# A macaron block on one core: the period of the first scores in an order of its own, and the first chunk's bias add and statistics moved

## The chip, the cores and the metric

The kernel runs on one core of a Trainium2 chip. The metric is the device time of one execution in microseconds (us); lower is better. Engines: PE (TensorE, matmuls), DVE (VectorE), ACT (ScalarE), POOL (GpSimd), and SP (SyncE), which here only issues DMAs. Each engine runs its own instructions strictly in their order; engines wait for each other on semaphores.

## The reference

The input x has 16 batches of 256 rows of 256 numbers. Three sublayers are added to it one after the other, each on the layer-normalised rows: half of a feed-forward, a causal attention with 16 heads of 16 and rotary positions, and half of the same feed-forward again.

```python
def ffn(x):                       # w1: 1024x256, w2: 256x1024, each quantised to -1, 0, 1
    h = gelu(x @ ternary(w1).T + b1)
    return h @ ternary(w2).T + b2
def ternary(w):                   # scale = mean(|w|), clip(round(w / scale), -1, 1)
    ...
x = x + 0.5 * ffn(layernorm(x))
x = x + attention(layernorm(x), Wq, Wk, Wv, Wo)      # softmax(rope(q) rope(k).T / 4, causal) v
x = x + 0.5 * ffn(layernorm(x))
```

## The kernel before, in words

All 4096 rows stay in SBUF in `res` (32 tiles of 128 rows). The kernel is three stages: feed-forward 0, attention, feed-forward 1.

**Feed-forward** goes by chunks of 512 rows. For a chunk, DVE makes `xn` (L147) from mean and rstd, which POOL works out in eight small instructions (`normaliser`, L116 to L132, called `moments`); PE transposes `xn` (L156), ACT and DVE split the transpose into a high and a low part (`xt_hi` L162, `xt_lo` L167), PE makes the hidden layer (L173) in 8 parts of 128 features, ACT applies gelu (L240), ACT or DVE rounds (`g_hi`), DVE takes the rest (`g_lo`, L257), and PE multiplies by `w2q` (L534): first for two of the four row tiles part by part as `g_lo` comes, then it transposes the next chunk's `xn`, then it does the other two tiles. POOL adds half of b2 to `res` (`residual`, L312); it may do so once the chunk's `xn` is made, and DVE adds PE's output only behind it.

**The first chunk** has the weights to quantise as well. DVE reduces |w1| (L344), PE spreads the mean over the partitions (`mean_of`, L497), DVE sets the threshold (L265, L267) and makes `w1q` in two halves (L355, L357), with `xt_lo` between them. ACT sums |w2| in four parts (L476); DVE adds these up (L362), waits for PE's second `mean_of`, which PE does behind the first two hidden parts, sets the second threshold, takes the statistics of chunk 1 (L142), and makes `w2q` in four pieces (L370, L372) between the first `g_lo`s. POOL waits for the first piece of `w1q`, does `residual(0)`, then `moments(1)`, then `residual(1)`.

**Attention** goes by periods p = -2, -1, 0, ..., 16, each in two halves h. Period p makes q and k of batch p+3 (`QK`, L670; `rope`, L677 and L680 on DVE; `rotate`, POOL L802; `top` L994, `take_rest` L889, `middle` L999 and `low` L807 split them into three bf16 parts, which SP stores to HBM, L686), makes v (`V`, L1158), normalises batch p+4 (`normalise`, L873; `XT`, L1171; `copy_xt`, L1008; `low_xt`, L912), makes the scores of batch p+1 only for their row maxima (`S`, 12 groups of L1057 and L1062 in a ring of three banks; `maxima`, DVE L860), splits and transposes the maxima (`split_max` POOL L789 to L795; `MT` PE L1138; `copy_max` ACT L1016; `max_rows` SP L756), and makes the scores of batch p again, transposed and with the maxima subtracted (`T`), with exponentials (L982) and the product with v (`PV`, L1118, L1121). SP loads q and k two periods ahead of `T` (`load`, L744), one half of the heads at a time, with `max_rows` and the stores in the same in-order queue. `normals` (POOL, the same eight instructions) serves two batches at once: it is done in every odd period behind `low`, from statistics that DVE takes in that period (L864). `MT` writes into the third bank of the scores' ring, so the next `S` in that bank waits for `copy_max`. The first scores are those of period -1 (`FIRST` is -2): there PE waits for their loads and only then goes on to `QK`.

Of the kernel before, what the change touches and what calls it, by code (L numbers as in the profile page):

```python
# [14 lines left out]
P = 128  # L15
# [3 lines left out]
FC = F // P  # L19
AHEAD, BEGUN = 7, 4  # L20
# [23 lines left out]
def macaron_kernel(nc, x, w1t, b1, w2t, b2, wqk, wv, wo, rope_cos, rope_sin, out):  # L44
    ctx = ExitStack()
    with ctx:
# [165 lines left out]
        def feed_forward(phase):  # L212
# [7 lines left out]
            with ExitStack() as stack:  # L220
# [78 lines left out]
                def gpsimd(pool):  # L299
                    if phase == 0:  # L300
                        constants(pool)
                        moments(pool, 0)
                        pool.wait_ge(bias_in, 32)
                        pool.tensor_scalar(b2h[:], b2f[:], 0.5, None, ALU.mult).then_inc(b2_ready, 1)

                        pool.wait_ge(b2_ready, 1)
                        pool.wait_ge(s_quant, 1)
# [8 lines left out]
                    if phase == 0:  # L316
                        moments(pool, 1)
                        residual(1)
                        for n, (hi, lo, full, _) in enumerate(att_weights):
                            pool.wait_ge(attw_hi, n + 1)  # L320
                            pool.tensor_tensor(lo[:], full[:], hi[:].bitcast(F32), ALU.subtract).then_inc(attw_lo, 1)
                        pool.wait_ge(attw_lo, len(att_weights))
# [13 lines left out]
                def vector(dve):  # L336
                    if phase == 0:
# [24 lines left out]
                        nc.vector.tensor_reduce(wtot[:, 1:2], wsum2[:], AX.X, ALU.add).then_inc(s_tot, 1)  # L362
                        threshold(1)
# [60 lines left out]
                    if phase == 0:  # L424
                        dve.wait_ge(x_in, 32)
                        ln_stats(1)
# [67 lines left out]
                def tensor(pe):  # L494
# [4 lines left out]

                    def first_qk(n):  # L500
                        pe.wait_ge(xt_hi_s, KC * n + KC)
                        pe.wait_ge(xt_lo_s, KC * n + KC)
                        for t in range(2):
                            qk_products(nc, banks[t], t, (wqk_hi, wqk_lo), [part[:, :, 0:SEQ] for part in (xt_hi, xt_lo)])\
                                .then_inc(turning.qk_ready, 1)
# [56 lines left out]
                    if phase == 0:  # L562
                        pe.wait_ge(const_ready, 15)
                        mean_of(0)
                        transpose_x(pe, 0)

# [124 lines left out]
def attention(nc, sem, banks, turning, res, wqk, wv, wo, cos_t, sin_t, ident, ident_b, mask_qk, mask_kq, minus_rows,  # L691
# [18 lines left out]
    with ExitStack() as ctx:  # L710
# [64 lines left out]
        def gpsimd(pool):  # L775
# [38 lines left out]
            def step(p, h):  # L814
                opening = p.known and p.p == FIRST
                if h == 0:
                    if opening:
                        normals(p)
                    if p.has(1):
                        pad(p)  # L820
                        split_max(p, 0)
                    if p.has(3):
                        rotate(p, 0)
                    if p.known and p.p == BATCH - 2:
                        moments(pool, following)
                else:
                    if p.has(3):
                        rotate(p, 1)
# [5 lines left out]
                    if p.par == 1 and p.has(5, 2, BATCH - 2) and not opening:  # L834
                        normals(p)
# [10 lines left out]
        def vector(dve, then):  # L846
# [74 lines left out]
            def step(p, h):  # L921
                opening = p.known and p.p == FIRST
                if p.has(1):
                    maxima(p, h)
                if h == 0:
# [3 lines left out]
                    if p.has(4, 2):  # L929
# [12 lines left out]
                    if p.has(3) and not opening:  # L942
# [3 lines left out]
                else:  # L946
                    if p.par == 1 and p.has(5, 2, BATCH - 2) and not opening:
# [12 lines left out]
                    if p.has(4, 2):  # L960
                        low_xt(p)
                    if p.has(-1):
# [7 lines left out]
        def scalar(act, then):  # L970
# [39 lines left out]
            def copy_max(p, h):  # L1010
# [5 lines left out]
                nc.scalar.copy(mt[h][:], mt_bank[0:PARTS * HALF, 0:SEQ // 2].bitcast(BF16)).then_inc(mt_sb, 1)  # L1016

            def step(p, h):
                if p.has(-1) if h == 0 else p.has(0):
# [33 lines left out]
        def tensor(pe):  # L1053
# [11 lines left out]
            def S(p, n):  # L1065
# [8 lines left out]
                if n % 6 == 2 and (p.has(0) or n > 2):  # L1074
# [60 lines left out]
            def MT(p, h):  # L1135
                pe.wait_ge(max_s, 4 * (2 * (p.p + 1) + h) + 4)
                for t in range(QT):
                    last = nc.tensor.transpose(mt_bank[:, t * P // 2:(t + 1) * P // 2].bitcast(BF16),  # L1138
                                               m_parts[:, t, :, :].rearrange("p a h -> p (a h)"), ident_b[:])
                last.then_inc(mt_ps, 1)  # L1140

# [54 lines left out]

            def step(p, h):
                closing = p.known and p.p == BATCH - 1
# [85 lines left out]
```

## Time and profile before

| | us |
|---|---|
| median of three runs (605.77 to 607.61) | 606.04 |
| the profiled execution's own time | 606.82 |
| its span | 605.1 |
| PE busy in it | 567.5 |
| DVE busy | 458.6 |
| ACT busy | 345.2 |
| POOL busy | 229.8 |

The span is the time from the first to the last instruction of the profiled execution. Busy time of PE is that of pipelined matmuls, whose ends are modelled. In the feed-forward 0 the first 32 us hold the first chunk's start; its last chunk ends near 153 us; the attention's period -1 lies between 160 and 180 us.

### The profile page before, as it was taken

The page shows a single profiled execution, that of the slowest core. Times are in us where ns is not written, and L with a number is a line of the kernel's source. Part 1 is how long each engine was busy: PE and PEld are TensorE (multiplying, and loading weights), DVE is VectorE, ACT ScalarE, POOL GpSimd, SP SyncE. Part 2 cuts the span into 40 slices and gives each one's busy share as a digit, 9 for nine tenths or more (in the row PEclk, how much of TensorE's full clock was granted, in tenths as well). Part 3 has the DMA queues.
Part 4 walks back from the last instruction along what each step waited for, and adds up shares of the span by engine and source line. Part 5 has one row for each costly group of instructions (what it writes and reads, how often), then busy time and mean ns, then how long its engine had stood idle before and what let it go on. Part 6 is the DMA issues. An engine that isn't in the chain of part 4 may idle for free.

```text
span 605.1 us, 17855 instructions
## 1 busy us (share of the span) xinstructions
PE 567.5 (94%) x6596; PEld 497.1 (82%) x6596; DVE 458.6 (76%) x928; ACT 345.2 (57%) x610; POOL 229.8 (38%) x446
## 2 busy tenths in 40 slices
PE   1899999999689999999999999999878999999997
PEld 1789999999668888888888888888665788899996
DVE  5977777778687988879878798877572777777764
ACT  1765455556236666866667666576556655554542
POOL 6373333333646353542545435434131033333310
PEclk9999999999889999999999999999999999999999
DMA  6630000000867666655575555766500011111111
GB/s 204 213 111 6 0 0 0 0 0 4 242 181 207 184 188 187 166 149 174 165 200 166 149 165 159 206 165 168 153 2 3 1 36 35 35 35 35 35 35 36
DMA packets 71142, 63.45 MB, mean 105 GB/s; under 512 B 4130, under 2 KB 64322, under 8 KB 71106
## 3 DMA queue, kind: packets, MB, share of 16 engines
q1 hardware_dynamic: 69922, 62.81, 35.9%
q8 instruction: 25, 0.41, 0.3%
q10 hardware_dynamic: 1184, 0.14, 0.2%
q14 instruction: 11, 0.09, 0.0%
HBM read 33.03 MB, written 29.36 MB: 103 GB/s over the span
## 4 chain that ended last, share of the span: by engine, by line
PE 82%; DVE 9%; DMA 3%; ACT 2%; POOL 2%; issue 1%; SPq 1%; DVEq 0%; POOLq 0%
PE bank L173 18%; PE bank L534 17%; PE bank L1062 13%; PE bank L670 7%; PE bank L1057 6%; PE bank L1118 5%; PE bank L1193 4%; PE bank L1158 3%; PE bank L156 2%; PE bank L1121 2%; PE bank L1131 2%; DVE mx L860 2%; DVE g_lo L257 1%; DMA w1f<-w1t 1%; PE bank L1181 1%
## 5 line engine op out<-in xcount | busy, mean ns | idle before, releaser
L860 DVE TENSOR_REDUCE mx<-bank 128x2 f32<-128x512 f32 (+1 forms) x192 | 118.4, 681 | 32.8 <-PE bank L1062 32.7
L534 PE MATMUL bank<-w2q,g_hi 128*128 128x256 f32 x512 | 124.4, 284 | 1.8 <-DVE g_lo L257 1.5
L240 ACT ACTIVATE g<-bank,b1c 128x512 f32<-128x512 f32 x128 | 88.1, 691 | 64.7 <-PE bank L173 61.5
L534 PE MATMUL bank<-w2q,g_lo 128*128 128x256 f32 x512 | 122.5, 280 | 0.0
L982 ACT ACTIVATE probs<-bank 128x512 f32<-128x512 f32 x192 | 111.1, 597 | 11.7 <-PE bank L1062 4.1
L534 PEld LDWEIGHTS bank<-w2q,g_hi 128*128 128x128 f32 x512 | 96.4, 188 | 3.6 <-DVE w2q L372 1.3
L534 PEld LDWEIGHTS bank<-w2q,g_lo 128*128 128x128 f32 x512 | 96.4, 188 | 0.6
L312 POOL TENSOR_TENSOR res<-res,b2h 128x1024 f32 (+1 forms) x16 | 38.4, 2400 | 133.2 <-DVE xn L147 128.6
L257 DVE TENSOR_TENSOR g_lo<-g,g_hi 128x512 fp32r<-128x512 f32 x128 | 82.6, 686 | 3.1
L173 PE MATMUL bank<-xt_hi,w1q 128*128 128x512 f32 x240 | 76.9, 402 | 2.0 <-DVE xt_lo L167 2.0
L173 PE MATMUL bank<-xt_lo,w1q 128*128 128x512 f32 x240 | 76.1, 398 | 0.0
L1062 PE MATMUL bank<-k,q 99*64 99x128 bf16 (+1 forms) x1024 | 75.2, 249 | 0.0
L1062 PE MATMUL bank<-q,k 102*64 102x256 bf16 (+1 forms) x1024 | 73.9, 245 | 0.0
L173 PEld LDWEIGHTS bank<-xt_lo,w1q 128*128 128x128 f32 x240 | 45.7, 190 | 10.9
L173 PEld LDWEIGHTS bank<-xt_hi,w1q 128*128 128x128 f32 x240 | 44.1, 191 | 12.0 <-issue 3.0
L1057 PE MATMUL bank<-mask_qk,ident_b 128*64 128x128 bf16 (+1 forms) x384 | 47.9, 245 | 6.2 <-DMA k<-qk_slots 3.2
L1057 PE MATMUL bank<-mask_kq,ident_b 128*64 128x128 bf16 (+1 forms) x384 | 47.9, 246 | 0.9 <-ACT probs L982 0.8
L802 POOL TENSOR_TENSOR rot<-by_cos,by_sin 128x512 f32<-128x512 f32 x30 | 38.4, 1282 | 25.7 <-DVE by_sin L680 24.1
L162 ACT CAST xt_hi<-bank 128x512 fp32r<-128x512 f32 x32 | 17.3, 589 | 52.6 <-PE bank L156 52.6
L248 DVE CAST g_hi<-g 128x512 fp32r<-128x512 f32 x60 | 25.5, 426 | 28.4 <-ACT g L240 26.9
L1016 ACT COPY mt<-bank 24x256 bf16<-24x256 bf16 x32 | 11.6, 362 | 61.6 <-PE bank L1138 61.1
L789 POOL TENSOR_TENSOR m_parts<-mx,zero 128x16 bf16<-128x16 f32 x32 | 8.3, 259 | 96.6 <-DVE mx L860 96.6
(129 smaller groups left out, 1172.6 us busy)
## 6 DMA issues: line engine op xcount, KB each, us to landing
qk_slots<-parts SPq DMA_DIRECT2D x32, 384.0 KB, 3.7
q<-qk_slots SPq DMA_DIRECT2D x32, 384.0 KB, 4.0
k<-qk_slots SPq DMA_DIRECT2D x32, 384.0 KB, 4.8
qk_slots<-parts SPq DMA_DIRECT2D x32, 256.0 KB, 3.4
res<-x SPq DMA_DIRECT2D x8, 512.0 KB, 3.6
qk_slots<-parts SPq DMA_DIRECT2D x32, 128.0 KB, 3.2
out<-res SPq DMA_DIRECT2D x8, 512.0 KB, 2.9
w1f<-w1t SPq DMA_DIRECT2D x2, 512.0 KB, 6.4
```

The costliest lines, as they stand in the source:

```text
L173: last = nc.tensor.matmul(to[:], w1q[:, k, f * P:(f + 1) * P], part[:, k, :], start=i == 0, stop=i == 2 * KC - 1)
L240: nc.scalar.activation(g[:, f, :], of[:], ACT.Gelu, bias=b1c[:, f:f + 1]).then_inc(g_ready, 1)
L257: nc.vector.tensor_tensor(g_lo[:, f, :], g[:, f, :], g_hi[:, f, :].bitcast(F32), ALU.subtract)\
L312: pool.tensor_tensor(res[:, bass.ts(c, CT), :], res[:, bass.ts(c, CT), :], b2h[:].unsqueeze(1).broadcast_to([P, CT, D]), ALU.add).then_inc ...
L534: last = nc.tensor.matmul(to[:, 0:D], part[:, f, t * P:(t + 1) * P], w2q[:, f, :], start=f == 0 and part is g_hi, stop=f == FC - 1 and par ...
L670: last = nc.tensor.matmul(to[:, e * SEQ:(e + 1) * SEQ], w[i][:, k, (2 * t + e) * P:(2 * t + e + 1) * P], x[a][:, k, :], start=n == 0, stop ...
L802: pool.tensor_tensor(rot[:, t, :], by_cos[:, t, :], by_sin[:, t, :], ALU.add).then_inc(rot_s, 1)
L860: nc.vector.tensor_reduce(o, i, AX.X, ALU.max).then_inc(s_done, 1)
L982: nc.scalar.activation(probs[g % 2][:, 512 * u:512 * u + 512], t_ring[n % 2][:], ACT.Exp, scale=0.25)\
L1057: nc.tensor.matmul(to[c, :, c], ident_b[:, c], mask[:, :, c], start=True, stop=False, skip_group_check=True)
L1062: last = nc.tensor.matmul(to[c, :], weights[:, c], moving, start=False, stop=stop, skip_group_check=True)
L1118: nc.tensor.matmul(o[32 * j:32 * j + 32, :], v_pad[par][:, 0, HALF * h + 4 * g + j, :], probs[g][:, j * SEQ:(j + 1) * SEQ], start=True, st ...
```

## The change

Six edits in two places.

First chunk (feed-forward 0): POOL no longer waits for `w1q`'s first half but for the last piece of `w2q` (`s_quant` 6), then does `moments(1)`, and only then `residual(0)`. DVE takes the statistics of chunk 1 between the sum of |w2| and the wait for its mean. PE issues 10 matmuls of 512 columns, whose result nobody reads, before the first `mean_of`, and 5 after the first transposes.

Period -1 of the attention: PE does 10 such matmuls, then `QK`, `S` 0 to 5, `V`, `XT`, `S` 6 to 11 and both `MT`s, all in place of `S` 0 to 5, `QK`, `MT`, `S` 6 to 11, `V`, `XT`, `MT`. DVE does `rope` and `normalise` ahead of `maxima`, and takes the statistics that period -1 took at the end of period -2. POOL does both `rotate`s before the first `split_max`, and its `normals` waits for period -1's `xn`. ACT does both `top`s, `copy_v`, `copy_xt`, both `copy_max`es and then both `middle`s. The first `MT` goes to another bank (`t_ring[1]`), and `S` 8 no longer waits for `copy_max`. SP is not changed.

```diff
+WARM = 10
 # gpsimd, phase 0
-                        pool.wait_ge(s_quant, 1)
+                        pool.wait_ge(s_quant, 6)
+                        moments(pool, 1)
...
                     residual(0)
                     if phase == 0:
-                        moments(pool, 1)
                         residual(1)
 # vector, phase 0
                         nc.vector.tensor_reduce(wtot[:, 1:2], wsum2[:], AX.X, ALU.add).then_inc(s_tot, 1)
+                        dve.wait_ge(x_in, 32)
+                        ln_stats(1)
                         threshold(1)
...
                     if phase == 0:
-                        dve.wait_ge(x_in, 32)
-                        ln_stats(1)
                         chunk(0, 1, 2)
 # tensor, phase 0
+                    def warm(times):
+                        for _ in range(times):
+                            nc.tensor.matmul(h_bank[3][:], ident_b[:], mask_qk[:].rearrange("p a k -> p (a k)"), start=True, stop=True)
...
                         pe.wait_ge(const_ready, 15)
+                        warm(WARM)
                         mean_of(0)
                         transpose_x(pe, 0)
+                        warm(WARM // 2)
 # attention, gpsimd step, h == 0 (second is p.p == FIRST + 1)
                     if p.has(1):
                         pad(p)
+                    if second:
+                        rotate(p, 0)
+                        rotate(p, 1)
+                    if p.has(1):
                         split_max(p, 0)
-                    if p.has(3):
+                    if p.has(3) and not second:
                         rotate(p, 0)
...
-                    if p.par == 1 and p.has(5, 2, BATCH - 2) and not opening:
+                    if p.par == 1 and p.has(5, 2, BATCH - 2):
+                        if second:
+                            pool.wait_ge(xn_s, 2 * QT)
                         normals(p)
 # attention, vector step
+                if second and h == 0:
+                    rope(p)
+                    normalise(p)
                 if p.has(1):
                     maxima(p, h)
...
                     if p.has(4, 2):
                         low_xt(p)
+                    if opening:
+                        statistics(p.turn(6))
 # attention, scalar
+            def second_step(p):
+                top(p, 0)
+                top(p, 1)
+                copy_v(p)
+                copy_xt(p)
+                copy_max(p, 0, t_ring[1])
+                copy_max(p, 1)
+                middle(p, 0)
+                middle(p, 1)
 # attention, tensor
-                if n % 6 == 2 and (p.has(0) or n > 2):
+                if n % 6 == 2 and p.has(0):
                     pe.wait_ge(mt_sb, 2 * b + n // 6)
...
+            def second_step(p):
+                pe_warm(WARM)
+                QK(p)
+                for n in range(6):
+                    S(p, n)
+                V(p)
+                XT(p)
+                for n in range(6, 12):
+                    S(p, n)
+                MT(p, 0, t_ring[1])
+                MT(p, 1)
```

## Rows read from the trace of the kernel before

**Rows 1.** The page's part 1: busy us, share of the span, instructions.

```profile
PE 567.5 (94%) x6596; PEld 497.1 (82%) x6596; DVE 458.6 (76%) x928; ACT 345.2 (57%) x610; POOL 229.8 (38%) x446
```

**Rows 2.** The chain that ended last, first 60 us: start, us, what.

```profile
15.74 3.75 PE bank L173 x8
...
20.09 1.31 DVE stats L142 x4
...
32.30 1.10 PE bank L156 x8
```

**Rows 3.** Timeline, first chunk: start, us, engine, line; in brackets idle before, releaser.

```profile
6.27 0.20 POOL L120 TENSOR_TENSOR both<-stats 128x8 f32<-128x8 f32 x1 [0.21 <-DVE stats L142]
...
9.03 0.86 POOL L304 TENSOR_SCALAR b2h<-b2f 128x256 f32<-128x256 f32 x1
...
11.98 1.97 PE L156 MATMUL bank<-ident,xn 128*128 128x128 f32 x8 [0.64 <-DVE xn L147]
...
12.22 0.75 DVE L355 TENSOR_SCALAR w1q<-w1f,thr 128x1024 fp32r<-128x1024 f32 x1
...
14.43 2.38 POOL L312 TENSOR_TENSOR res<-res,b2h 128x1024 f32<-128x1024 f32 x1 [4.54 <-DVE w1q L357]
...
15.41 1.96 DVE L355 TENSOR_SCALAR w1q<-w1f,thr 128x1024 fp32r<-128x1024 f32 x1
...
17.67 20.68 SPq L273 DMA_DIRECT2D res<-x  x6
...
19.75 0.16 DVE L265 TENSOR_SCALAR thr<-bank 128x1 f32<-128x1 f32 x1 [1.00 <-PE bank L497]
...
21.32 0.47 DVE L370 TENSOR_SCALAR w2q<-w2f,thr 128x512 fp32r<-128x512 f32 x1
...
21.48 0.37 POOL L120 TENSOR_TENSOR both<-stats 128x8 f32<-128x8 f32 x1 [4.67 <-DVE stats L142]
...
25.75 0.47 POOL L132 TENSOR_TENSOR rstd<-rstd 128x4 f32<-128x4 f32 x1
...
26.59 0.75 DVE L372 SCALAR_TENSOR_TENSOR w2q<-w2f,thr,w2q 128x512 fp32r<-128x512 f32 x1
...
27.26 3.69 DVE L257 TENSOR_TENSOR g_lo<-g,g_hi 128x512 fp32r<-128x512 f32 x6
```

**Rows 4.** The same timeline, window from 30.8 us.

```profile
30.87 1.37 DVE L147 TENSOR_SCALAR xn<-res,mean,rstd 128x256 f32<-128x256 f32 x4
```

**Rows 5.** The chain that ended last, 160 to 212 us.

```profile
167.11 4.29 PE bank L670 x24
...
183.07 3.06 PE bank L670 x24
```

**Rows 6.** PE by windows: length, PE busy (count), granted clock, DMA share, GB/s.

```profile
163.00:164.00 1.00, 0.51 (x9) 0.50 1.01 270
...
169.00:170.00 1.00, 1.00 (x7) 0.59 0.52 145
```

**Rows 7.** Timeline of PE, 146 to 193 us.

```profile
163.49 0.42 PE L1057 MATMUL bank<-mask_qk,ident_b 128*64 128x256 bf16 x2 [3.24 <-DMA k<-qk_slots]
...
180.32 0.25 PE L1057 MATMUL bank<-mask_qk,ident_b 128*64 128x128 bf16 x2 [1.14 <-ACT mt L1016]
...
187.99 0.22 PE L1057 MATMUL bank<-mask_kq,ident_b 128*64 128x128 bf16 x2
```

**Rows 8.** Timelines of DVE, POOL and SP, 146 to 193 us.

```profile
157.51 2.03 DVE L873 TENSOR_SCALAR xn<-res,mean,rstd 128x256 f32<-128x256 f32 x2
...
172.69 3.67 DVE L860 TENSOR_REDUCE mx<-bank 128x4 f32<-128x512 f32 x6
...
184.07 0.98 DVE L873 TENSOR_SCALAR xn<-res,mean,rstd 128x256 f32<-128x256 f32 x2 [0.36 <-POOL rstd L132]
...
183.97 0.61 POOL L781 COPY v_pad<-v_all 128x512 f32<-128x512 f32 x1
...
184.80 0.74 SPq L756 DMA_DIRECT2D q<-mt  x1
```

More of the change, by code:

```diff
@@ L814, in step @@
             def step(p, h):
-                opening = p.known and p.p == FIRST
+                opening, second = p.known and p.p == FIRST, p.known and p.p == FIRST + 1
                 if h == 0:
@@ L826, in step @@
                 else:
-                    if p.has(3):
+                    if p.has(3) and not second:
                         rotate(p, 1)
@@ L921, in step @@
             def step(p, h):
-                opening = p.known and p.p == FIRST
+                opening, second = p.known and p.p == FIRST, p.known and p.p == FIRST + 1
+                if second and h == 0:
+                    rope(p)
+                    normalise(p)
                 if p.has(1):
@@ L928, in step @@
                         rope(p)
-                    if p.has(4, 2):
+                    if p.has(4, 2) and not second:
                         normalise(p)
@@ L941, in step @@
                         ln_stats(1)
-                    if p.has(3) and not opening:
+                    if p.has(3) and not opening and not second:
                         rope(p)
@@ L946, in step @@
                 else:
-                    if p.par == 1 and p.has(5, 2, BATCH - 2) and not opening:
+                    if p.par == 1 and p.has(5, 2, BATCH - 2) and not second:
                         statistics(p.turn(5))
@@ L1008, in copy_xt, with copy_max @@
                 nc.scalar.copy(xt[p.parity(4)][0], mixed[0][:].rearrange("p (k n) -> p k n", k=KC)).then_inc(xt_hi_s, 1)
-            def copy_max(p, h):
+            def copy_max(p, h, of=mt_bank):
                 act.wait_ge(mt_ps, 2 * (p.p + 1) + h + 1)
@@ L1015, in copy_max @@
                     act.wait_ge(m_loaded[p.parity(0)][h], 16 * (p.turn(0) + 1))
-                nc.scalar.copy(mt[h][:], mt_bank[0:PARTS * HALF, 0:SEQ // 2].bitcast(BF16)).then_inc(mt_sb, 1)
+                nc.scalar.copy(mt[h][:], of[0:PARTS * HALF, 0:SEQ // 2].bitcast(BF16)).then_inc(mt_sb, 1)
+            def second_step(p):
[7 more added lines that the diff above has]
+                middle(p, 1)
             def step(p, h):
+                if p.known and p.p == FIRST + 1:
+                    if h == 1:
+                        second_step(p)
+                    return
                 if p.has(-1) if h == 0 else p.has(0):
@@ L1133, in OT, with MT, pe_warm @@
                 last.then_inc(turned, 1)
-            def MT(p, h):
+            def MT(p, h, to=mt_bank):
                 pe.wait_ge(max_s, 4 * (2 * (p.p + 1) + h) + 4)
                 for t in range(QT):
-                    last = nc.tensor.transpose(mt_bank[:, t * P // 2:(t + 1) * P // 2].bitcast(BF16),
+                    last = nc.tensor.transpose(to[:, t * P // 2:(t + 1) * P // 2].bitcast(BF16),
                                                m_parts[:, t, :, :].rearrange("p a h -> p (a h)"), ident_b[:])
                 last.then_inc(mt_ps, 1)
+            def pe_warm(times):
+                for _ in range(times):
+                    nc.tensor.matmul(t_ring[0][:], ident_b[:], mask_qk[:].rearrange("p a k -> p (a k)"), start=True, stop=True)
             def QK(p):
@@ L1195, in WO @@
                 last.then_inc(wo_ready, 1)
+            def second_step(p):
[9 more added lines that the diff above has]
+                MT(p, 1)
             def step(p, h):
+                if p.known and p.p == FIRST + 1:
+                    if h == 1:
+                        second_step(p)
+                    return
                 closing = p.known and p.p == BATCH - 1
```

## The prediction

> **What bounds the kernel now.** I read the busy shares first: PE is busy 567.5 of 605.1 us [rows 1], so a cut elsewhere pays only where PE waits for it. Then the chain of waits for the two places that the diff touches, because there PE does wait. In the first chunk the chain runs over DVE: two hidden parts at a slow pace (8 matmuls in 3.75 us), the statistics, `w2q` and `g_lo`, `xn`, and from the transposes at 32.30 on PE alone [rows 2]. Whatever comes later at 32.30 comes later at the end, and likewise for earlier. In the attention the chain runs over the loads of q and k, a slow `QK` (4.29 us for 24 matmuls, against 3.06 one period later) [rows 5], and the maxima, and PE takes over at 180.32 behind `copy_max` [rows 7]. The timelines of DVE, POOL and SP give who holds whom, the windows the granted clock.
>
> **Edit 1, POOL's bias add moved.** Before, `residual(0)` runs 14.43 to 16.81, and DVE's second L355, issued at 15.41, takes 1.96 us where the first took 0.75 [rows 3]. It is held until about 16.6. The same shows at `xn` of period -2 (2.03 us for two instructions beside two `rotate`s, against 0.73 where alone: half of the four at 30.87 less one overlap) and at 184.07, where `xn` waits for POOL's rstd, POOL starts its next instruction at 183.97, ahead of DVE, and `xn` takes 0.98 [rows 4, 8]. So a DVE instruction of this kind stands still while a POOL instruction of some size runs, and POOL's next instruction gets in ahead of a DVE that waits for its rstd. Removing the hold on L355 gains 1.96 - 0.75 = 1.2.
>
> **Edit 2, statistics into the wait for the mean.** DVE waits 1.00 for PE's mean (L265 at 19.75) and then takes the statistics in 1.31 [rows 2, 3]. Now the 1.31 covers the wait, if the mean comes within them. The gain is 1.0 at most. The data are there: SP's next load of x, which waits for the same semaphore, is issued at 17.67 [rows 3], and the new place is at about 17.5, so I take 0 to 0.2 for a wait on it.
>
> **Edit 3, PE warmed at the start.** It decides only whether the mean comes in time. L173 runs at 0.47 per matmul at the start, and the first 8 transposes take 1.97 where the later 8 take 1.10 [rows 2, 3], which is the lower of the two clock levels (1.2 and 2.4 GHz). At full pace the two hidden parts would end near 17.7 instead of 19.5, and the mean would be hidden. If the warming fails, its five matmuls behind the transposes (about 0.43 each by the slow L173) end near 16.1 and delay the hidden parts by up to 0.4; the mean then comes as late as now, or 0.4 later, and edit 2 gains 0.1 to 0.3 instead of 1.0. I take the full 1.0: with transposes and warming PE is busy without a break from 11.98.
>
> Edits 1 to 3 bring `w2q` from 21.32 to about 19.1 (2.2 earlier). Its last piece ends at 27.34 - 2.2 = 25.1, and the last `g_lo`, which ended at 27.26 + 3.69 = 30.95 [rows 3], ends at 28.75.
>
> **What the moved bias add meets.** Now POOL starts `moments(1)` at 25.1. Alone the eight instructions take 6.27 to 9.03 = 2.8 us, beside DVE's work 21.48 to 26.22 = 4.7 [rows 3]. Six `g_lo`s stand beside them, so I take the upper end, less a little for the last instructions, which run when DVE is idle: done at 29.65. Before, rstd was ready 4.7 us ahead of its use; now `xn(1)` waits 0.9 for it. And behind rstd POOL holds `residual(0)`, 2.38 us, with nothing left to wait for. By the row pair at 183.97 and 184.07 it gets in first, and holds `xn` until about 29.6 + 2.2 = 31.8. Four `xn`s of 1.37 end at 33.2; before they ended at 32.24 [rows 4]. So the transposes start 0.9 later: 2.2 gained, 0.9 lost waiting for rstd, 2.2 lost behind the bias add. Bounds: if the moments take 2.8, the bias add holds `g_lo` or `xn` all the same but nothing waits for rstd, +0.1; if `xn` gets in ahead of it, 29.7 + 1.3 = 31.0, -1.2; if the mean is late as well, +1.7. `residual(1)` stays behind `xn` and keeps its cover.
>
> The Trainium skill (SBUF — State Buffer, SBUF: two separate sides) states the same as a rule: GpSimd and VectorE share a pair of ports under an exclusive lock, for the whole instruction, against a VectorE operation in a two-port mode or with two SBUF inputs. The trace agrees for L355 and `xn`. For `g_lo`, which has two SBUF inputs, no row shows a large POOL instruction beside it; by the rule the bias add holds it too, which is the +0.1 case, and without the rule that case would be -1.2.
>
> **PE's clock in that hole.** The first half of the output matmuls ends 0.9 behind the last `g_lo`, at about 29.7; the transposes come at 33.2. PE stands idle some 3.5 us, where it stood 0.5. The nearest row is the idle of 3.24 before 163.49, behind which the granted clock was 0.50 and came back only at about 169.6 [rows 6, 7]. The stretch at the start (3.75 us at half pace) lost 1.9, that in the attention 6.2 us long up to 3.1; PE is the bound from there, so all of it counts. From 0 (kept) to 3.1; weighing the two I take 1.6. First chunk: +0.9 + 1.6 = +2.5.
>
> **Edit 4, period -1.** Before, PE idles 3.24 for the loads, then runs `S` and `QK` at half clock. Now the ten warming matmuls (about 0.22 each, the full-pace size) fill 160.3 to 162.4, where `xt_lo` is ready, and `QK` (24 matmuls, 3.0) ends at 165.4 with the loads landed. DVE does `rope` to 166.8 and `xn` beside POOL's second `rotate`, 1.6 by the 2.03 row less what is past: to 168.4. `maxima` 0 to 5 take 3.67 [rows 8], to 172.1. PE does `S` 0 to 2 by 166.4, waits for the first maximum until 169.1, does `S` 3 to 5 sparsely to 170.6, `V` and `XT` to 172.4, and `S` 6 at 172.8; `maxima` 6 to 11 end at 176.5, `split_max` at 177.5, `MT` and `copy_max` at 178.3. Before, `copy_max` let `S` go on at 180.32 [rows 7]: 2.0 gained there, 1.3 of it the statistics moved into the idle DVE of period -2.
>
> Two things take it back. SP's queue: `max_rows` of the second half stands behind the six stores, which wait for `low`; `middle` now stands behind both `copy_max`es and begins at 178.2 as before, so the stores and the `max_rows` at 184.80 [rows 8] stay. `T` 6 needs that row; before it ran at 187.99 [rows 7]. It cannot be earlier than 184.80 plus a landing, at most 3.2 by this pair and at least the 0.74 of its issue. POOL's `normals` also stays behind `low`, so `xn` stays at 184.07. PE's lead at `T` 6 is then 0 to 1.2, I take 0.7. The first `max_rows` is issued at 175.7 instead of 171.9, with the second load behind it; both have over 2 us in hand.
>
> The other is the clock: PE has 2.7 us idle from 166.4 and then 1 us of work in 4. If the clock falls there, `V`, `XT` and `S` 6 take 2 us more, the maxima, `middle`, stores and `normals` all come about 2 later than now, and `T` 6 slips to some 1.3 behind. Between -0.7 and +1.3 I take -0.3: the idle is shorter than the 3.24 that lost the clock.
>
> The Trainium skill (TensorE: Matmul & The Clock Gate, HAM oscillation — how this bites in real kernels) states that waits between bursts bring the lower clock back each time. That speaks against this change: it closes one hole before `QK` and opens one in each place. The trace agrees by the 0.50 behind the 3.24 us.
>
> **Sum.** +0.9 + 1.6 - 0.3 = +2.2. Against the profiled execution's 606.82 (span 605.1 and 1.7 around it) that is 609.0; that execution lies 0.8 above the median, so against 606.04 I forecast **608.2**.
>
> **Rivals and chances.** A measurement of this kernel tells 0.3%, about 1.8 us, from no change: 604.2 and 607.9 are the bounds.
> - Forecast, the bias add in front of `xn` opens a hole and the clock falls in it (606.6 to 611.0, of which 608.2 is the middle): 0.42. For it: the three held DVE instructions and the 3.24 us row.
> - The hole opens but the clock holds: +0.9 - 0.3 = +0.6, 606.6; with the +0.1 case 605.8. For it: the length of the hole is a difference of estimates, and `g_lo`s held one by one would split it. 0.27.
> - The clock falls in both places: +0.9 + 3.1 + 1.3 = +5.3, 611.3. 0.10.
> - Other side: POOL's bias add does not get ahead of `xn` (place: rstd's release at 29.65; it decides as soon as DVE's first `xn` is started before POOL's L312), and both clocks hold: -1.2 - 0.7 = -1.9, 604.1; with the whole 2.0 of period -1 kept, -3.2, 602.8. For it: DVE stands ready at rstd. Against it: the pair at 184. 0.21.
>
> Faster by over 0.3%: 0.19. Within: 0.36 (the second case, and a part of the first and last). Slower: 0.45. The range leaves out half of the last case and a few of the third: 603.8 to 611.2; the forecast case's own is 606.6 to 611.0.
>
> **What would show it.** In the timeline after: L355 at 0.75 twice (edit 1); no idle before the second L265 (edits 2, 3), `w2q` from about 19.1; L120 at about 25.1; L312 started before the first L147 of chunk 1, which takes over 2 us; PE idle over 3 us before the transposes, and L534 or L156 at double length behind it. In period -1: `QK` in 3.0 us, `copy_max` near 178.3, L756 still near 184.8 and `T` 6 near 187.3, all shifted by the first part. The prediction is wrong if L147 of chunk 1 starts ahead of L312, or if the granted clock stays at 1.00 across both holes.

## The result and the profile after

The changed kernel takes 612.73 us (median of 4), the one before 606.25: ratio 1.0107, 95% interval 1.0084 to 1.0129, slower by 6.5 us. I had forecast 608.2, slower. The direction and the loss in the first chunk are as forecast. The loss in period -1, for which I had -0.3, is not, and 612.73 lies outside the range.

The first chunk in the timeline of the changed kernel (start, us, engine, line; in brackets the idle before and its releaser). The lines moved by one to six: L356 was L355, L373 L370, L258 L257, L148 L147, L314 L312, L157 L156, L540 L534.

```profile
5.06 3.73 PE L504 MATMUL bank<-mask_qk,ident_b 128*128 128x512 bf16 x10 [5.06 <-POOL mask_kq L202]
...
11.87 1.97 PE L157 MATMUL bank<-ident,xn 128*128 128x128 f32 x8 [0.91 <-DVE xn L148]
...
15.29 0.74 DVE L356 TENSOR_SCALAR w1q<-w1f,thr 128x1024 fp32r<-128x1024 f32 x1
...
17.39 1.41 DVE L143 BATCH_NORM_STATS2 stats<-res 128x6 f32<-128x256 f32 x4
...
18.72 0.14 DVE L266 TENSOR_SCALAR thr<-bank 128x1 f32<-128x1 f32 x1
...
19.08 0.49 DVE L373 TENSOR_SCALAR w2q<-w2f,thr 128x512 fp32r<-128x512 f32 x1
...
25.03 3.70 DVE L258 TENSOR_TENSOR g_lo<-g,g_hi 128x512 fp32r<-128x512 f32 x6
...
25.26 0.52 POOL L121 TENSOR_TENSOR both<-stats 128x8 f32<-128x8 f32 x1 [15.43 <-DVE w2q L375]
...
29.99 0.20 POOL L133 TENSOR_TENSOR rstd<-rstd 128x4 f32<-128x4 f32 x1
30.14 2.34 POOL L314 TENSOR_TENSOR res<-res,b2h 128x1024 f32<-128x1024 f32 x1
30.23 3.37 DVE L148 TENSOR_SCALAR xn<-res,mean,rstd 128x256 f32<-128x256 f32 x4 [1.49 <-POOL rstd L133]
...
33.65 1.97 PE L157 MATMUL bank<-ident,xn 128*128 128x128 f32 x8 [4.05 <-DVE xn L148]
...
35.63 0.41 PE L540 MATMUL bank<-w2q,g_lo 128*128 128x256 f32 x1
```

Against [rows 3, 4]: L356 takes 0.74 where it took 1.96 (edit 1), L266 waits for nothing (edit 2), `w2q` starts at 19.08 instead of 21.32 (2.2, as summed). Then POOL's `moments(1)` runs from 25.26 to 30.19, its bias add starts at 30.14, DVE's first `xn` at 30.23, and the four `xn`s take 3.37 instead of 1.37. PE idles 4.05, and behind it the transposes take 1.97 instead of 1.10 and the output matmuls 0.41 instead of 0.28 each. The chain of waits says the same for the whole of them (start, us, what):

```profile
30.23 0.04 DVE xn L148
30.26 2.28 issue
32.55 1.06 DVE xn L148 x3
...
33.65 1.97 PE bank L157 x8
35.62 5.18 PE bank L540 x32
```
The chain of the kernel before:

```profile
33.40 3.81 PE bank L534 x32
```

The same 32 matmuls took 3.81 there. The transposes start 1.35 later than in [rows 2], and 0.87 and 1.37 are added behind them: 3.6 us.

The granted clock of PE (window, length, busy and matmuls, granted clock, DMA share, GB/s):

```profile
12.00:14.00 2.00, 2.00 (x9) 0.50 0.93 287
...
36.00:38.00 2.00, 2.00 (x12) 0.50 0.59 208
...
40.00:42.00 2.00, 2.00 (x13) 1.00 0.43 151
...
172.00:174.00 2.00, 1.37 (x20) 0.50 0.56 168
...
182.00:184.00 2.00, 0.00 (x0) 1.00 0.18 29
...
186.00:188.00 2.00, 2.00 (x30) 0.50 0.35 88
```

0.50 is the lower of the two levels, 1.2 GHz. Apart from the start it stands behind the idle of 4.05 in the first chunk, behind one of 2.63 in period -1 and, from about 185.4 us, behind one of 3.00 at its end:

```profile
163.85 2.11 PE L1178 MATMUL bank<-mask_qk,ident_b 128*128 128x512 bf16 x9
165.86 0.51 PE L678 MATMUL bank<-xt_hi,wqk_hi 128*128 128x256 f32 x2
...
172.63 0.42 PE L1090 MATMUL bank<-mask_qk,ident_b 128*64 128x256 bf16 x2 [2.63 <-DVE mx L874]
...
174.50 0.80 PE L1196 MATMUL bank<-wv_hi,xt_hi 128*128 128x256 f32 x2
...
184.58 0.28 PE L1171 MATMUL bank<-ident_b,m_parts 128*128 128x128 bf16 x2 [3.00 <-POOL m_parts L803]
...
194.79 0.30 PE L1090 MATMUL bank<-mask_qk,ident_b 128*64 128x256 bf16 x2
```

L1178 are the warming matmuls, L1090 the first matmuls of an `S`, L1196 `V`, L1171 an `MT`. DVE in the same stretch of the changed kernel (L874 `maxima`, L887 `xn`, L903 `take_rest`):

```profile
170.30 1.68 DVE L887 TENSOR_SCALAR xn<-res,mean,rstd 128x256 f32<-128x256 f32 x2
171.90 3.66 DVE L874 TENSOR_REDUCE mx<-bank 128x4 f32<-128x512 f32 x6
178.95 3.68 DVE L874 TENSOR_REDUCE mx<-bank 128x4 f32<-128x512 f32 x6 [3.39 <-PE bank L1095]
182.55 1.30 DVE L903 TENSOR_TENSOR rest<-rot,parts 128x512 f32<-128x512 f32 x2
```
POOL in the kernel before, then here (L789 and L797 are the first instruction of `split_max`):

```profile
176.44 0.22 POOL L789 TENSOR_TENSOR m_parts<-mx,zero 128x16 bf16<-128x16 f32 x1 [2.32 <-DVE mx L860]
```
```profile
182.71 0.60 POOL L797 TENSOR_TENSOR m_parts<-mx,zero 128x16 bf16<-128x16 f32 x1 [5.96 <-DVE mx L874]
```
SP's queue there (both `max_rows`):

```profile
182.00 0.75 SPq L764 DMA_DIRECT2D q<-mt  x1
...
191.62 0.74 SPq L764 DMA_DIRECT2D q<-mt  x1
```

`xn` meets the second `rotate`, the second six maxima wait 3.39 for `S` 6, `take_rest` stands right behind them beside `split_max`, and the second `max_rows` is issued at 191.62 where it was 184.80 [rows 8]. The `S` that ran at 187.63 before runs at 194.79: 7.16 later, of which 3.57 were there when the attention began. So period -1 cost 3.6 as well. The spans of the two profiles differ by 7.1 (612.2 and 605.1), and from 210 to 600 us PE is busy for 380.4 us against 380.1 before: what is lost up to there is not given back.

### The profile page after: what moved, and what is told of

Its sections match the earlier page's. It is cut to its first block, busy times and chain, and to the rows that moved or that the text cites. A ratio compares the mean times of both kernels' runs of the same rounds, so it can differ in the third digit from the quotient of the medians.

```text
span 612.2 us, 17903 instructions
## 1 busy us (share of the span) xinstructions
PE 576.6 (94%) x6620; PEld 501.7 (82%) x6621; DVE 461.2 (75%) x928; ACT 345.5 (56%) x610; POOL 228.8 (37%) x446
## 4 chain that ended last, share of the span: by engine, by line
PE 85%; DVE 8%; POOL 2%; issue 2%; ACT 1%; DMA 1%; SPq 0%; DVEq 0%; POOLq 0%
PE bank L540 19%; PE bank L174 18%; PE bank L1095 13%; PE bank L678 8%; PE bank L1090 6%; PE bank L1151 5%; PE bank L1231 4%; PE bank L1196 3%; PE bank L157 3%; PE bank L1154 2%; PE bank L1164 2%; DVE mx L874 2%; PE bank L1209 1%; DMA w1f<-w1t 1%; PE bank L1219 1%
## 5 line engine op out<-in xcount | busy, mean ns | idle before, releaser
L874 DVE TENSOR_REDUCE mx<-bank 128x2 f32<-128x512 f32 (+1 forms) x192 | 118.8, 682 | 36.1 <-PE bank L1095 36.0
L540 PE MATMUL bank<-w2q,g_hi 128*128 128x256 f32 x512 | 125.8, 286 | 1.5 <-DVE g_lo L258 1.1
L540 PE MATMUL bank<-w2q,g_lo 128*128 128x256 f32 x512 | 123.7, 282 | 0.0
L540 PEld LDWEIGHTS bank<-w2q,g_hi 128*128 128x128 f32 x512 | 97.6, 191 | 3.3 <-DVE w2q L375 1.2
L540 PEld LDWEIGHTS bank<-w2q,g_lo 128*128 128x128 f32 x512 | 97.5, 191 | 0.6
L314 POOL TENSOR_TENSOR res<-res,b2h 128x1024 f32 (+1 forms) x16 | 38.3, 2392 | 126.7 <-DVE xn L148 126.7
L258 DVE TENSOR_TENSOR g_lo<-g,g_hi 128x512 fp32r<-128x512 f32 x128 | 82.6, 686 | 3.2
L1090 PE MATMUL bank<-mask_qk,ident_b 128*64 128x128 bf16 (+1 forms) x384 | 47.9, 246 | 3.7 <-DVE mx L874 3.5
L1090 PE MATMUL bank<-mask_kq,ident_b 128*64 128x128 bf16 (+1 forms) x384 | 48.2, 248 | 0.9 <-ACT probs L1001 0.8
L810 POOL TENSOR_TENSOR rot<-by_cos,by_sin 128x512 f32<-128x512 f32 x30 | 38.5, 1284 | 25.5 <-DVE by_sin L688 24.1
L797 POOL TENSOR_TENSOR m_parts<-mx,zero 128x16 bf16<-128x16 f32 x32 | 8.5, 266 | 100.0 <-DVE mx L874 100.0
L1095 PEld LDWEIGHTS bank<-k,q 99*64 99x64 bf16 x1024 | 44.5, 112 | 0.2
```

Of the source, the lines that this page charges most:

```text
L258: nc.vector.tensor_tensor(g_lo[:, f, :], g[:, f, :], g_hi[:, f, :].bitcast(F32), ALU.subtract)\
L314: pool.tensor_tensor(res[:, bass.ts(c, CT), :], res[:, bass.ts(c, CT), :], b2h[:].unsqueeze(1).broadcast_to([P, CT, D]), ALU.add).then_inc ...
L540: last = nc.tensor.matmul(to[:, 0:D], part[:, f, t * P:(t + 1) * P], w2q[:, f, :], start=f == 0 and part is g_hi, stop=f == FC - 1 and par ...
L810: pool.tensor_tensor(rot[:, t, :], by_cos[:, t, :], by_sin[:, t, :], ALU.add).then_inc(rot_s, 1)
L874: nc.vector.tensor_reduce(o, i, AX.X, ALU.max).then_inc(s_done, 1)
L1090: nc.tensor.matmul(to[c, :, c], ident_b[:, c], mask[:, :, c], start=True, stop=False, skip_group_check=True)
```

## The experiments

Each was timed against the kernel before on the same chip (605.3 to 605.7 us there). Single executions of a kernel lie 1 to 4.5 us apart, so differences are read from the ratios, whose intervals reach 0.8 to 1.5 us to either side. "Filled" means that unread (warming) matmuls of 512 columns stand where PE would be idle (in a hole).

| run | what | ratio, 95% interval | us against before |
|---|---|---|---|
| a_first | first chunk's edits alone | 1.0067, 1.0043 to 1.0092 | +4.1 |
| h_first_filled | the same, hole filled | 1.0032, 1.0019 to 1.0046 | +1.9 |
| g_no_bias | the same, no bias add there | 1.0015, 0.9998 to 1.0033 | +0.9 |
| c_keep_bias | the same, bias add not moved | 0.9980, 0.9965 to 0.9995 | -1.2 |
| e_bias_in_stats | bias add beside the statistics | 0.9976, 0.9964 to 0.9989 | -1.5 |
| b_att | period -1's edits alone | 1.0065, 1.0040 to 1.0091 | +3.9 |
| d_att_filled | the same, holes filled | 1.0031, 1.0018 to 1.0044 | +1.9 |
| l_scores_ahead | filled, S 6 to 8 ahead of V | 1.0022, 1.0009 to 1.0035 | +1.3 |
| n_v_last | hole behind S 2 filled, V and XT behind S 11 | 1.0019, 1.0001 to 1.0037 | +1.2 |
| o_v_last_middle | and middle ahead of copy_max | 1.0050, 1.0037 to 1.0064 | +3.0 |
| f_wait_filled | old order, wait filled | 0.9983, 0.9969 to 0.9997 | -1.0 |
| i_wait_filled_stats | and statistics early | 0.9966, 0.9952 to 0.9981 | -2.1 |
| m_after_filled | the change, all holes filled | 1.0047, 1.0034 to 1.0061 | +2.8 |
| j_both | e and i together | 0.9947, 0.9926 to 0.9969 | -3.2 |

**The two places apart.** `a_first` is the kernel before with the first chunk's edits, `b_att` with those of period -1.

> The kernel before with the first chunk's edits alone (bias add behind the quantisation of w2, statistics in the wait, both warmings of PE). Theory: in the changed kernel the transposes of chunk 1 started 1.35 later than before (33.65 against 32.30), they took 1.97 instead of 1.10 and the 32 output matmuls behind them 5.18 instead of 3.81, so 1.35 + 0.87 + 1.37 = 3.6 us slower, 609.9. Rival: the first chunk's loss is given back or absorbed by the attention's start (PE waits there for loads), then under 1 us slower.

> The kernel before with the edits of period -1 alone. Theory: the other half of the loss is made here, through two falls of the granted clock, +3.6 us, 609.9; as much as 1 us less or more, since the clock may fall at another moment. Rival: the second place lost only because it started from a disturbed first; then within 0.7 us of before, as my prediction had it (-0.3).

+4.1 and +3.9: each place loses by itself, and both rivals (absorbed by the attention's start; lost only from a disturbed start) fall. Together they give 8.0 where the change lost 6.5; the intervals, some 1.5 us on either side of each, cover that.

**The bias add.** `c_keep_bias` leaves POOL as it was; `g_no_bias` has nothing in its place:

```diff
-                    residual(0)
+                    if phase == 0:
+                        pool.sem_inc(xb_ready, 1)
+                    else:
+                        residual(0)
```

`e_bias_in_stats` puts it where DVE takes the statistics, with `moments(1)` behind:

```diff
-                        pool.wait_ge(s_quant, 1)
+                        pool.wait_ge(s_tot, 2)
```

> The first chunk's edits without the move of the bias add (which stands where it stood before); attention as before. Theory (the moved bias add is the whole of the first chunk's loss): L355 is held again, 1.96 us, but the wait for the mean is covered and no hole opens before the transposes: w2q starts 1.0 earlier than before, so -1.0 us, 605.2, and no clock below 1.00 between 18 and 160 us. Rival (the warming or the early statistics cost something themselves): slower than before or the same.

> The first chunk's edits without the bias add of chunk 0 (chunk 0's rows of the output lack b2 of the first feed-forward); moments(1) still behind the quantisation of w2. Theory (the port holds xn for 2.3, and the hole it opens loses the clock): xn waits only for rstd, to about 30.2, takes 1.37, transposes at 31.6, 0.7 before the 32.30 of the kernel before, PE idles 2.1 there and keeps its clock: -0.7 us against before, 4.8 below the kernel with the bias add there. Rival (the wait for rstd is the larger part, or the hole of 2.1 already loses the clock): slower than before, +1 to +2.

> The first chunk's edits, but POOL's bias add waits for DVE's sum of |w2| (s_tot 2) in place of the last piece of w2q, with moments(1) behind it; attention as before. It then stands beside the statistics and the wait for the mean, where DVE holds and needs no shared port. Theory (the bias add costs what DVE instructions it meets): L355 takes 0.75, the bias add from 17.4 to 19.8 holds only the first w2q piece by 0.5, moments end by 25: 1.2 + 1.0 - 0.5 = 1.7 us faster than before, 603.7, and 0.6 faster than the kernel that keeps it in place (-1.1 measured). Rival (first w2q piece waits for the whole bias add and the pieces behind meet the moments): no better than -1.1.

With POOL's work unmoved the loss of 4.1 turns into a gain of 1.2: moving the bias add and `moments(1)` is the whole loss of the first chunk. Without the bias add POOL is just as late with rstd, and `xn` takes its 1.38 (timeline of `g_no_bias`):

```profile
13.66 1.28 DVE L168 TENSOR_TENSOR xt_lo<-bank,xt_hi 128x512 fp32r<-128x512 f32 x2
...
29.89 0.20 POOL L133 TENSOR_TENSOR rstd<-rstd 128x4 f32<-128x4 f32 x1
...
30.13 1.38 DVE L148 TENSOR_SCALAR xn<-res,mean,rstd 128x256 f32<-128x256 f32 x4 [1.49 <-POOL rstd L133]
...
31.56 1.09 PE L157 MATMUL bank<-ident,xn 128*128 128x128 f32 x8 [2.07 <-DVE xn L148]
```

The profiled executions come to this place up to 0.7 us apart, so I measure from the start of `xt_lo` (L168) to the transposes: before 14.21 to 32.30 = 18.09; after 19.56; here 31.56 - 13.66 = 17.90. So the bias add's hold makes 1.7 (19.56 - 17.90) of the change's delay, and the 1.5 us that DVE waits for rstd alone is less than what edits 1 and 2 had gained. Here PE idles 2.07 and its clock stayed at 1.00 in the profile, with which the profiled execution took 604.65; the ten executions lie between 604.20 and 608.72, and their mean granted clocks go with that: 0.992 to 0.997 in the three under 605, 0.985 to 0.989 in the four over 606.9 (though one of 606.37 has 0.997). So the median of +0.9, against the -0.2 of the trace, is probably made by executions that lost the clock somewhere; that it was in this hole no trace shows, and another place is possible (the last section). My expectation of -0.7 was too good.

In `e_bias_in_stats` the bias add meets one piece of `w2q`:

```profile
13.53 1.28 DVE L168 TENSOR_TENSOR xt_lo<-bank,xt_hi 128x512 fp32r<-128x512 f32 x2
...
17.00 2.39 POOL L313 TENSOR_TENSOR res<-res,b2h 128x1024 f32<-128x1024 f32 x1 [6.86 <-DVE wtot L363]
...
18.76 0.92 DVE L373 TENSOR_SCALAR w2q<-w2f,thr 128x512 fp32r<-128x512 f32 x1
...
23.63 0.47 POOL L133 TENSOR_TENSOR rstd<-rstd 128x4 f32<-128x4 f32 x1
...
28.75 1.38 DVE L148 TENSOR_SCALAR xn<-res,mean,rstd 128x256 f32<-128x256 f32 x4
...
30.18 1.09 PE L157 MATMUL bank<-ident,xn 128*128 128x128 f32 x8 [0.50 <-DVE xn L148]
```

L373 takes 0.92 instead of 0.49, rstd is ready at 24.1, `xn` waits for nothing: 16.65 from `xt_lo` to the transposes, 1.44 less than before, and -1.5 in the time (-1.7 expected).

**The hole in the first chunk.** 18 warming matmuls ahead of the transposes:

```diff
+                        if first:
+                            warm(18)
                         if more and not closing:
                             transpose_x(pe, n + 1)
```

> The first chunk's edits with the bias add moved, and 18 unread matmuls of 512 columns (some 3.9 us) between the first half of chunk 0's output and the transposes of chunk 1. Theory: the 4.05 us hole is filled, the granted clock stays at 1.00, transposes take 1.1 and the 32 output matmuls 3.8; only the late xn is left, +1.35 us against before, 606.8. Rival (the slow matmuls behind the hole wait for something else): over +3 stays.

+4.1 becomes +1.9 (1.35 expected). The transposes take 1.10 and start 19.85 behind `xt_lo`, 1.8 later than before. So of the first chunk's loss about 2.2 is the clock and the rest the late `xn`.

**Period -1: clock and order.** `d_att_filled` puts 11 warming matmuls behind `S` 2 and 11 between the `MT`s; `m_after_filled` is the whole change with these and the 18 of the first chunk; `f_wait_filled` leaves the old order and puts 14 ahead of its first `S`:

```diff
 # d_att_filled, second_step
                 for n in range(6):
                     S(p, n)
+                    if n == 2:
+                        pe_warm(11)
...
                 MT(p, 0, t_ring[1])
+                pe_warm(11)
                 MT(p, 1)
 # f_wait_filled, PE's step of the kernel before
+                if p.known and p.p == FIRST + 1 and h == 0:
+                    pe_warm(14)
```

> The period -1 edits alone, with 11 more unread matmuls of 512 columns behind S 2 and 11 between the two MTs, where PE stands idle 2.6 and 3.0 us. Theory (the clock makes the loss): the granted clock stays at 1.00 from 150 to 200 us, V takes 1.4 instead of 2.86, and of the +3.6 between 2.7 and 4.1 come back: -0.5 to +0.9 us against before. Rival (the order itself makes the loss, DVE's maxima and the wait of MT for split_max): more than +2 us stays.

> The kernel before, in its old order everywhere, with 14 unread matmuls of 512 columns in the wait for the loads ahead of the first scores. Theory (clock): S and QK of period -1 run at the full clock, QK's 24 matmuls take 3.0 instead of 4.29, DVE's rope and everything behind it come 1.3 earlier, 1.3 us faster, 604.1. Rival (what follows is bound by DVE and the stores, not by QK): under 0.4 us faster.

> The changed kernel with its three holes filled (18 unread matmuls ahead of chunk 1's transposes, 11 behind S 2, 11 between the MTs), all else as changed. Theory: of the 6.5 us the clock makes 2.5 to 3, the orders the rest: 2.0 (first chunk filled) + 1.9 (period -1 filled) = +3.9 against before, 609.3, granted clock 1.00 from 20 us on. Rival (the changed kernel's loss is the order's alone): over +5.5.

Filling takes 2.0 of the 3.9 back; 1.9 stays, more than the upper end that I gave by 1.0. In the old order the same idea gains 1.0 (1.3 expected): `QK` runs at the full pace. The changed kernel with all three holes filled still loses 2.8 of its 6.5 (3.9 expected), so the clock made about 3.7. The other 2.8 are the late `xn` of the first chunk and the order of period -1.

The kernel before loses the clock in period -1 too, behind its wait for the loads, and the traces show what that hides. From the last transposes of period -2 to the first `PV` of period 0's second half they take 35.22 before, 33.09 in the old order filled (`f_wait_filled`), and 36.22 in the new order filled (`d_att_filled`). So the new order costs 3.1 at the full clock; 2.1 of it is made up because the change also closes the hole ahead of `QK`.

**What of the order.** `l_scores_ahead` takes `S` 6 to 8 ahead of `V` and `XT`; `n_v_last` takes both behind `S` 11 (with 11 warming matmuls behind `S` 2 only); `o_v_last_middle` also puts `middle` around `copy_xt`, ahead of `copy_max`.

```diff
 # n_v_last, second_step
-                V(p)
-                XT(p)
                 for n in range(6, 12):
                     S(p, n)
+                V(p)
+                XT(p)
 # o_v_last_middle, ACT
+                middle(p, 0)
                 copy_xt(p)
+                middle(p, 1)
                 copy_max(p, 0, t_ring[1])
                 copy_max(p, 1)
-                middle(p, 0)
-                middle(p, 1)
```

> The changed kernel's period -1 with both holes filled, and S 6 to 8 ahead of V and XT. Theory (of the +1.9 that the filled order kept, 1.3 is DVE standing idle for V and XT between the two runs of maxima): DVE goes from one run to the other without idle, +0.6 us against before, 606.0. Rival (middle behind copy_max, or split_max beside take_rest, keeps it): +1.5 or more stays.

> The changed kernel's period -1 with the hole behind S 2 filled, and V and XT behind S 11, where the kernel before has them, ahead of the two MTs; first chunk as before. Theory (V and XT ahead of any S stop DVE for as long as they take, 1.27 to 1.29 in both orders tried): DVE takes the twelve maxima in one run, split_max, copy_max, middle and the stores come 1.3 earlier than with V in the middle; +1.9 - 1.3 = +0.6 us against before. Rival (the rest of the order, middle behind copy_max above all, makes the +1.9): +1.3 or more stays.

> The same with ACT's two middles ahead of both copy_maxes, as the kernel before has them. Theory: middle and with it low, the stores and normals come 1.5 to 2 earlier, as rest is done long before the second MT; the time falls below before, -0.5 to -1.0 us. Rival (POOL's low, 2.3 us, then stands in front of the maxima's way out, or the loads set the pace): the same as with middle behind copy_max.

DVE's maxima of period -1 (x is how many), first in `d_att_filled`:

```profile
167.27 3.67 DVE L867 TENSOR_REDUCE mx<-bank 128x4 f32<-128x512 f32 x6
172.22 3.68 DVE L867 TENSOR_REDUCE mx<-bank 128x4 f32<-128x512 f32 x6 [1.29 <-PE bank L1088]
```
In `l_scores_ahead`, nine and three:

```profile
168.04 5.46 DVE L867 TENSOR_REDUCE mx<-bank 128x4 f32<-128x512 f32 x9
174.77 1.89 DVE L867 TENSOR_REDUCE mx<-bank 128x4 f32<-128x512 f32 x3 [1.27 <-PE bank L1088]
```
In `n_v_last`, all twelve in one run:

```profile
167.59 7.25 DVE L867 TENSOR_REDUCE mx<-bank 128x4 f32<-128x512 f32 x12
```

The idle of 1.3 moves with `V` and `XT` and goes only when they stand behind the last `S`. So my expectation for `l_scores_ahead`, no idle and +0.6, was wrong; +1.3 came. To put both behind the last `S` is worth 0.7 by the medians, 1.1 by the traces (over the same stretch 36.22 in `d_att_filled`, 35.14 in `n_v_last`). Then another wait stands in its place, for the first half's row of maxima: its `MT` now stands behind `V` and `XT` as well, POOL begins the second `split_max` only behind it, and SP issues the row only behind `copy_max`. PE in `n_v_last` (L1164 is the second `MT`, L1083 the first instruction of a `T`):

```profile
177.07 0.28 PE L1164 MATMUL bank<-ident_b,m_parts 128*128 128x128 bf16 x2 [1.34 <-POOL m_parts L796]
...
178.66 0.25 PE L1083 MATMUL bank<-mask_kq,ident_b 128*64 128x128 bf16 x2 [0.85 <-DMA q<-mt]
```
The same instructions in `o_v_last_middle`:

```profile
177.45 0.28 PE L1164 MATMUL bank<-ident_b,m_parts 128*128 128x128 bf16 x2 [1.31 <-POOL m_parts L796]
...
180.09 0.32 PE L1083 MATMUL bank<-mask_kq,ident_b 128*64 128x128 bf16 x2 [1.90 <-DMA q<-mt]
```
PE by windows in `o_v_last_middle` (window, length, busy, granted clock):

```profile
175.00:180.00 5.00, 1.88 (x23) 0.85 0.05 11
180.00:185.00 5.00, 4.91 (x62) 0.50 1.04 309
```

With `middle` ahead, `copy_max` and so the row come later, PE idles 1.90 for it instead of 0.85, and the clock falls again (0.50 from 180 us). Over the same stretch the trace is 3.4 longer than that of `n_v_last` (38.53 against 35.14): 1.0 is the later row, 2.4 the slow matmuls behind it (5.84 from this `T` to `QK`, against 3.44). So my expectation for `o_v_last_middle`, a gain, was wrong in sign. Whether `middle` ahead would pay with this hole filled was not run.

In the trace period -1 of `n_v_last` is no longer than that of the kernel before (35.14 against 35.22), though the medians have it at +1.2. Of its ten executions the two with a mean clock of 1.000 took 605.93 and 605.94, the six with 0.996 took 606.68 to 607.07, and the two with 0.993 took 608.98 and 609.25. In the profiled execution, one of the six, the clock fell near 444 us, behind the attention's last waits, and not in period -1. So a part of the +1.2 goes with a clock that was lost somewhere; how much of it is the order's is not shown. Against the old order filled (33.09) this order is still 2.1 longer.

**The statistics.** `i_wait_filled_stats` adds to `f_wait_filled` only the statistics at the end of period -2 and POOL's wait for `xn`; `j_both` puts that and `e_bias_in_stats` in one kernel.

```diff
 # i_wait_filled_stats, vector; the same condition leaves period -1's own statistics out
                         low_xt(p)
+                    if opening:
+                        statistics(p.turn(6))
 # gpsimd
-                    if p.par == 1 and p.has(5, 2, BATCH - 2) and not opening:
+                    if p.par == 1 and p.has(5, 2, BATCH - 2):
+                        if p.known and p.p == FIRST + 1:
+                            pool.wait_ge(xn_s, 2 * QT)
```

> The old order with the wait for the loads filled (14 unread matmuls), and of the changed kernel's period -1 only one edit: DVE's statistics at the end of period -2, with POOL's normals waiting for period -1's xn. Theory: DVE stands idle there, so 1.3 us leave the chain from the maxima to middle, copy_max, the stores and normals, on top of the 0.8 that filling gave: 2.1 us faster than before, 603.2; the second MT and copy_max come 1.3 earlier in the trace. Rival (split_max meets take_rest at the shared port, as in the changed kernel, and gives it back): 0.8 to 1.2 faster only.

> The first chunk with the bias add beside the statistics, and period -1 in its old order with the wait filled and the statistics early. Theory: the two places are independent and what is gained in each stays: 1.7 + 2.1 = 3.8 us faster than before, 601.6. Rival (the second place is reached earlier but waits for something that does not move): 1.7 to 2.5 faster.

-2.1 and -3.2. In `i_wait_filled_stats` the second `MT` is late as the rival says (`split_max` meets `take_rest`, first instruction 0.60 instead of 0.22), but `low`, `normals` and the stores are early. The -2.1 is the number that I expected, but the traces split it otherwise than I did: over the stretch of above filling alone saves 2.1 (33.09 against 35.22) and the statistics 0.4 more (32.73), where I had 0.8 and 1.3, so that the number came out right is in part luck. How much is the statistics' own is not settled. `j_both` has a time of 602.82 against 605.70, the fastest kernel of this study; its interval, 0.9926 to 0.9969 (-4.5 to -1.9 us), holds the sum of the two (-3.5) and my -3.8, but does not shut out the rival's 1.9 to 2.5 either.

## Why the prediction was wrong

**Edits 1 to 3: right.** 2.2 us earlier `w2q` was forecast, 21.32 - 19.08 = 2.2 came; `c_keep_bias` and `e_bias_in_stats` show that they are worth having when the bias add stands elsewhere. The warming reached the hidden parts (0.62 to 0.64 for two from 16.18), but not all of it did: the first eight transposes still take 1.97, at a granted clock of 0.50 from 12 to 14 us. So the ten matmuls ahead of `mean_of` did nothing for the transposes, and whether the five behind the transposes would have done alone was not run.

**The moved bias add: right in kind, 1.35 instead of 0.9.** POOL did get in ahead of DVE at rstd (30.14 and 30.23), and held `xn` 2.0 longer than its own 1.37. `moments(1)` took 4.93, not 4.55: I had shortened it for the time in which DVE idles.

**The clock in that hole: right that it fell, 2.24 instead of 1.6.** I took a middle between kept and fallen. An execution has one side or the other and not the middle; 0.87 for the transposes and 1.37 for the 32 matmuls behind them, the first part of them at half pace, are what the fallen one cost.

**Period -1: the step that failed.** I priced it at -0.3, "the idle is shorter than the 3.24 that lost the clock". That took the length of one idle for a limit, which no row showed. The idle was 2.63, the clock fell at once (0.50 at 172 us), and the term measured +3.6 in the trace and +3.9 in `b_att`. The sentence before that had the right working for this case (`V`, `XT` and `S` 6 at half pace, maxima and stores 2 later), but +1.3 as its end was too small, for three reasons. The fall leads to a second idle of 3.00 before the last `MT`, which lost the clock again while `S` and `T` of period 0 are bound by PE; I had seen only the first. `split_max` takes 1.8 instead of 1.1, because `take_rest` stands right behind the maxima, where the statistics had stood between them: its first two instructions take 0.60 and 0.54 beside `take_rest`, here and in `b_att`, `d_att_filled` and `i_wait_filled_stats`, and 0.22 to 0.25 without it, before and in `n_v_last`. That is a hold between POOL and DVE as in the first chunk, which I had applied there and not here. And `V` and `XT` ahead of `S` 6 stop DVE; my own schedule put 0.7 of idle there, it is 1.3 even at the full clock.

**What decided for the range.** The case with the clock fallen in both places stood in the text at +5.3, 611.3, with a chance of 0.10. It is what happened, and at +6.5: its first chunk was put at +4.0 and came at +3.6, its period -1 at +1.3 and came at +3.6. The range was also too short by its own sums: it ended at 611.2, just below the 611.3 of that case, and so left out half of the case or more, not "a few". And 608.2 is not the middle of 606.6 to 611.0, which is 608.8. Neither of my two signs of being wrong came: one looks at the first chunk, the other at a clock that stays up in both places, and none at a fall in period -1.

## What to carry to other kernels

Before a large instruction of POOL is moved, list the DVE instructions that it will meet in the new place, and look above all at the one that waits for POOL's own result: here POOL's next instruction got in first. An idle stretch of PE can have two prices, its length and the slow matmuls behind it; sum the fallen case to its end, with the waits that it makes late, and don't take the shortest idle that has lost the clock so far for a limit. Where the wait can't be closed, unread matmuls in it took back 1.0 to 2.2 us here. Independent work of PE between two runs of an engine that feeds on PE costs that engine time: `V` and `XT`, some 1.9 us long, left DVE idle for 1.3.

## What the runs showed of the hardware that was not expected

The granted clock fell behind or in idle stretches of 4.05, 3.00 and 2.63 us, and in `g_no_bias` it stayed up across 2.07 in the profiled execution. The length of one idle does not decide it alone: in `o_v_last_middle` the clock fell in the second of two idles of 1.31 and 1.90 with 0.7 us of work between.

There is a third place, which no edit touched. At the end of the attention, between 439 and 452 us, PE waits 1.09 for an `MT` and 0.54 for a `PV`, in every kernel. In the profiled executions of `a_first`, `b_att`, `f_wait_filled` and `n_v_last` the clock fell to 0.50 behind these two; in the other twelve it stayed at 1.00. From the `PV` of period 0's second half to the end these four take 410.76 to 411.03 us, the twelve 410.03 to 410.29. So a fall there costs about 0.7, and two single executions can differ by that much whatever was changed.

At the start the clock's rows can't be trusted. In the profile of the kernel before they say 1.00 from 12 to 20 us, where the first eight transposes take 1.97 and the hidden parts run at half pace; in that of `m_after_filled` they say 1.00 from 0 to 20 us, and its transposes take 1.97 too. There the pace of the matmuls is the better witness.

Single times of the kernel before lie 3.7 us apart on one chip (31 executions, 603.83 to 607.55), those of `m_after_filled`, whose granted clock is 1.00 in the stretches from 20 to 500 us of its profile, 1.0 (ten, 608.53 to 609.54). The other kernels with every long idle of their period -1 filled lie between: 1.0 (`l_scores_ahead`), 1.6 (`d_att_filled`), 2.0 (`f_wait_filled`) and 2.6 (`i_wait_filled_stats`). That filling makes the time steadier is likely by this, and not shown.
